# A second set of buffers for the turned probabilities, used in alternate steps

## The chip, the cores and the metric

The kernel runs on one core of a Trainium2 chip, as one launch. The metric is the device time of that core in microseconds (us), median of three runs. Lower is better.

## The reference, cut to what matters

The reference is a stack of four gated layers on a state x of 8 sequences of 112 tokens with 256 channels. Each layer does x = x + tanh(g) * attention(layernorm(x)) and then x = x + tanh(g) * ffn(layernorm(x)). The attentions look at a context of 375 tokens for each sequence:

```python
scores = q @ k.T * scale            # per head, 112 x 375
probs  = softmax(mask(scores))      # rows sum to one
out    = (probs @ v) @ w_o
```

- layer 0 (`a0`): 8 heads of 32 channels
- layer 1 (`a1`): 1 head of 128 channels
- layer 2 (`a2`): 16 heads of 16 channels; its feed-forward part holds two more self-attentions over the 112 tokens themselves (`af[0]`, `af[1]`), 16 heads of 16, causal, each followed by a mixture of experts
- layer 3 (`a3`): 16 heads of 64 channels

Everything is float32 except a quantized feed-forward part at the end. The feed-forward parts are not touched by the change.

## The kernel before, in words

The eight sequences are taken four at a time: four `LANES` (j = 0 to 3) make one iteration, and each attention runs two iterations (`it`). Every engine has its own program, and the order of work on each is written out by hand; semaphores (named `probs`, `probs_turned`, `probs_T`, ...) tie the engines together. An engine does its instructions strictly in the order written, so an instruction that waits holds back all that stand behind it on that engine.

An attention is cut into `tiles` of 128 channels (m), and a tile into `steps` (s); r = m * steps + s counts the steps through. One step takes one head of each of the four lanes (two heads a lane in `af`). The cross attentions have the following shapes: `a0` has 2 tiles of 4 steps, `a1` 1 tile of 1 step, `a2` 2 tiles of 8 steps, `a3` 8 tiles of 2 steps. Each `af` has 2 tiles of 4 steps. The work of a step r goes through these stations:

1. TensorE, `scores_of(r)` (L544): queries times keys, into PSUM banks 0 to 3, one for each lane.
2. VectorE, `mask_and_min(r)` (L668): adds the mask, writes the masked scores to SBUF (into `E` in even steps, `E_odd` in odd ones, so this buffer is already double) and finds the row minimum of the negated scores.
3. ScalarE, `exps(r, j)` (L749): the exponential in place, with the row sums.
4. TensorE, `turn_probs(r)` (L560): transposes the probabilities, 12 transposes of 112 x 125 (8 of 112 x 112 in `af`), into PSUM banks 4 to 6 (4 and 5 in `af`). It waits until the banks of step r - 1 were emptied.
5. ScalarE, `keep_probs(r)` (L761, in `af` L758), and VectorE, `keep_rest(r)` (L683): copy the turned probabilities from PSUM to SBUF, into `PT`. ScalarE takes two thirds of them (two copies of 125 x 448; one of 112 x 448 in `af`), VectorE the rest (one copy).
6. TensorE, `outputs_of(r)` (L584): turned probabilities times values, into PSUM bank 7. Its last matmul signals `probs_used`.

There is a single `PT`. So both copies of step r wait at station 5 for two signals: `probs_turned(r)`, and `probs_used(r - 1)`, which says that TensorE has read the turned probabilities of the step before.

The order on TensorE inside a tile is `outputs_of(r - 2)`, `scores_of(r + 1)`, `turn_probs(r)`, for each step (L602 to L609). In the last step of a tile it is `outputs_of(r - 2)`, then keys and queries of the next tile for two lanes (L491), `turn_probs(r)`, `outputs_of(r - 1)`, keys and queries for the other two lanes, `outputs_of(r)`, and the values of the next tile; in the last tile of an attention there is no next tile, and `turn_probs(r)`, `outputs_of(r - 1)`, `outputs_of(r)` follow each other with nothing between. After it come `turn_sums` (L592), the copy of the inverse row sums (L767), the scaling (L697) and the output projection (L491).

The order on ScalarE in a step is `exps(r, 0)`, `exps(r, 1)`, `keep_probs(r - 1)`, `exps(r, 2)`, `exps(r, 3)` (L773 to L781); in the last step of a tile `keep_probs(r)` stands behind them. The order on VectorE is `keep_rest(r - 1)`, `mask_and_min(r + 1)` (L709 to L712).

The buffers lie in one large SBUF tensor, `arena`, 4864 words for each lane, in which names share space when they are not in use at the same time; `stream` is a second tensor of 8192 words that holds weights in the expert stages, and in `a2` the values split by parity of the head (`V_keys`, its first 3072 words).

Of the kernel before, what the change touches and what calls it, by code (L numbers as in the profile page):

```python
# [28 lines left out]
S2 = 375  # L29
P = 128  # L30
# [62 lines left out]
class Attention:  # L93


    def __init__(self, tiles, heads, d, keys, key_tiles, wq, wk, wv, bq=None, bk=None, bv=None,
                 mask=None, guard=False, masked=None, by_parity=None, q_rows=None):
        self.tiles, self.heads, self.d, self.keys, self.key_tiles = tiles, heads, d, keys, key_tiles
        self.key_w = keys // key_tiles

        self.strip = max(32, d)
        self.strips = P // self.strip
        self.paired = d < 32
        self.whole_pairs = self.paired and key_tiles == 1
        self.group = 2 if self.whole_pairs else 1
        self.steps = heads // self.group
        self.stay = 2 if self.paired and not self.whole_pairs else 1
        self.wq, self.wk, self.wv, self.bq, self.bk, self.bv = wq, wk, wv, bq, bk, bv
        self.mask, self.guard, self.scale = mask, guard, float(d) ** -0.5
        self.masked, self.by_parity, self.q_rows = masked, by_parity, q_rows  # L110
# [16 lines left out]
def flamingo(nc, A, out):  # L127
    ctx = ExitStack()
    with ctx:
# [137 lines left out]
        PT_all, spread_all = lanes[:, :, off["p"]:off["p"] + 4 * T], lanes[0:T, :, off["s"]:off["s"] + P]  # L267
# [65 lines left out]

        def no_mask(j):
            return zero_col[0:T, :].broadcast_to([T, S2])

        a0 = Attention(2, 4, 32, S2, KEY_TILES, w_q0, w_k0, w_v0, "l0_bq", "l0_bk", row("l0_bv", KEY_W),
                       mask=no_mask, masked=twice)
        a1 = Attention(1, 1, 128, S2, KEY_TILES, w_q1, w_k1, w_v1, "l1_bq", "l1_bk", row("l1_bv", KEY_W),
                       mask=lambda j: maskb[0], guard=True, masked=twice)  # L340
        a2 = Attention(2, 8, 16, S2, KEY_TILES, w_q2, w_k2, w_v2, "l2_bq", "l2_bk", row("l2_bv", KEY_W),
                       mask=lambda j: maskb[j], masked=twice,
# [3 lines left out]
                        masked=lambda r, j: E[j][:, r % 2 * 2 * T:r % 2 * 2 * T + 2 * T], by_parity=V_rows)  # L346
              for l in range(2)]
        a3 = Attention(8, 2, 64, S2, KEY_TILES, w_q3, w_k3, w_v3, mask=no_mask, masked=twice)
# [155 lines left out]
        def attend_tensor(pe, a, p, it, rx, keys_of, keys_ready):  # L504
# [59 lines left out]
            def outputs_of(r):  # L564
# [10 lines left out]
                for first in range(0, LANES, a.strips):  # L575
                    for i in range(n):
                        for j in range(first, min(first + a.strips, LANES)):
                            t, rows = 0 if a.whole_pairs else i, a.rows(s, j)
                            if a.paired:
                                e, f = a.odd(s, i), t * P + rows.start  # L580
                                v = a.by_parity[j][0:a.key_w, e, f:f + a.strip]
                            else:
                                v = V[j][0:a.key_w, t, rows]
                            last = pe.matmul(outs[rows, j * T:(j + 1) * T], v, PT[j][0:a.key_w, i * T:(i + 1) * T],  # L584
                                             start=(i == 0 and s % a.stay == 0),
                                             stop=(i == n - 1 and s % a.stay == a.stay - 1))
# [43 lines left out]
        def attend_vector(v, a, p, it):  # L630
# [42 lines left out]
            def keep_rest(r):  # L673

                v.wait_ge(*p["probs_turned"].at(it, r))
                if r:
                    v.wait_ge(*p["probs_used"].at(it, r - 1))
                if a.whole_pairs:
                    dst, src = PT_all[0:T, 2:4, 0:2 * T], three(bank[5][0:T, 0:4 * T], 2)
                else:  # L680
                    n = a.key_tiles - 1
                    dst, src = PT_all[0:a.key_w, :, n * T:(n + 1) * T], three(bank[4 + n][0:a.key_w, 0:LANES * T], LANES)
# [48 lines left out]
        def attend_scalar(act, a, p, it):  # L731
# [21 lines left out]
            def keep_probs(r):  # L753
                act.wait_ge(*p["probs_turned"].at(it, r))
                if r:
                    act.wait_ge(*p["probs_used"].at(it, r - 1))
                if a.whole_pairs:
                    last = act.copy(PT_all[0:T, 0:2, 0:2 * T], three(bank[4][0:T, 0:4 * T], 2))  # L758
                else:
                    for t in range(a.key_tiles - 1):  # L760
                        last = act.copy(PT_all[0:a.key_w, :, t * T:(t + 1) * T],  # L761
# [1319 lines left out]
```

## Time and profile before

| | |
|---|---|
| median of 3 runs | 1913.39 us (1908.18 to 1920.59) |
| the profiled execution | 1915.56 us, of which the span of its instructions 1913.8 us |
| mean granted TensorE clock | 0.884 of full speed |
| TensorE busy (matmul) | 1534.9 us, 80% of the span |
| VectorE busy | 803.4 us, 42% |
| ScalarE busy | 674.3 us, 35% |
| GpSimd busy | 215.3 us, 11% |

The shares are means over stages that differ. By the trace the attentions lie as follows: `a0` from about 43 to 92 and 176 to 224 us, `a1` between 328 and 405, `a2` from 583 to 668 and 679 to 766, `af[0]` from 786 to 829 and 868 to 912, `af[1]` from 1162 to 1206 and 1252 to 1295, `a3` from 1446 to 1622 and 1642 to 1818 us. All the rest is projections, norms, experts and feed-forward parts. In rows of the timeline a bracket tells how long the engine had been idle before the instruction, and what ended the idle time.

### The profile page before, as it was taken

What the parts mean: (1) busy time and instruction counts of PE and PEld (TensorE: products, weight loads), DVE (VectorE), ACT (ScalarE), POOL (GpSimd) and SP (SyncE); (2) the same over time, 40 slices, a digit from 0 to 9 for tenths busy, and PEclk for the clock granted to TensorE, in tenths of its full rate; (3) what the DMA queues carried; (4) which work ended last, traced back from release to release, by engine and by line L of the source; (5) the groups of instructions that cost most, each with busy time, mean ns of one, the idle gap of its engine ahead of it and who ended that gap; (6) DMA issues with size and microseconds to landing.
All of it is one profiled execution on the core that took longest, in us unless ns stands there. A gap on an engine that the chain in (4) does not pass through costs nothing.

```text
span 1913.8 us, 34703 instructions
## 1 busy us (share of the span) xinstructions
PE 1534.9 (80%) x11511; PEld 1245.6 (65%) x11511; DVE 803.4 (42%) x2884; ACT 674.3 (35%) x2117; POOL 215.3 (11%) x326
## 2 busy tenths in 40 slices
PE   5977767879889889758469966487998999999954
PEld 4666655768776666536358955366896777787733
DVE  3545445441116565656301126563004443344456
ACT  2513413232106656426023325262333444244411
POOL 0000000000001111111221122014500000000000
PEclk9988988889999999867579988587999999999977
DMA  9300000128601100400169830112951001000000
GB/s 351 117 1 1 0 4 32 33 99 285 182 6 48 48 2 2 158 1 1 66 226 351 300 131 21 46 44 99 319 199 33 2 2 33 2 1 1 2 0 20
DMA packets 103092, 156.23 MB, mean 82 GB/s; under 512 B 12199, under 2 KB 80928, under 8 KB 102248
## 3 DMA queue, kind: packets, MB, share of 16 engines
q1 hardware_dynamic: 97355, 143.53, 22.7%
q0 software_dynamic: 3552, 9.18, 1.4%
q10 hardware_dynamic: 2048, 1.84, 0.3%
q8 instruction: 70, 1.15, 0.2%
q14 instruction: 67, 0.54, 0.1%
HBM read 147.31 MB, written 11.67 MB: 83 GB/s over the span
## 4 chain that ended last, share of the span: by engine, by line
PE 74%; DVE 8%; issue 6%; ACT 4%; DMA 4%; POOL 3%; SPq 1%; DVEq 1%; ACTq 0%; POOLq 0%
PE psum L491 51%; PE psum L560 8%; PE psum L584 6%; PE psum L544 5%; ACT arena L749 2%; DMA moe_b<-in_moe_b 2%; PE psum L479 2%; ACT arena L761 1%; SPq L889 1%; POOL rstd L461 1%; POOL stream L1111 1%; PE psum L592 1%; POOL token_rows L1083 1%; DMA region<-in_l_wv 1%; DVE x_state L823 1%
## 5 line engine op out<-in xcount | busy, mean ns | idle before, releaser
L491 PE MATMUL psum<-region,arena 128*125 128x128 f32 (+4 forms) x2160 | 372.7, 327 | 50.0 <-DVE arena L697 15.7
L491 PEld LDWEIGHTS psum<-region,arena 128*125 128x125 f32 (+2 forms) x2160 | 304.3, 191 | 113.5 <-issue 24.9
L749 ACT ACTIVATE arena<-arena,rowmin 112x375 f32<-112x375 f32 (+1 forms) x584 | 292.1, 505 | 187.4 <-DVE rowmin L668 187.1
L491 PE MATMUL psum<-arena,region 128*128 128x112 f32 (+2 forms) x1984 | 347.2, 335 | 4.2 <-DVE x_state L1738 1.7
L491 PEld LDWEIGHTS psum<-arena,region 128*128 128x128 f32 x1984 | 283.4, 205 | 69.3 <-issue 12.2
L560 PE MATMUL psum<-identity,arena 112*125 112x112 f32 (+1 forms) x1240 | 177.7, 287 | 30.9 <-ACT arena L761 14.8
L560 PEld LDWEIGHTS psum<-identity,arena 112*125 112x125 f32 (+1 forms) x1240 | 145.0, 180 | 87.1 <-ACT arena L761 26.6
L479 PE MATMUL psum<-identity,arena 112*128 112x112 f32 x176 | 39.0, 391 | 148.1 <-DVE arena L471 96.6
L491 PE MATMUL psum<-arena 128*128 128x128 f32 (+4 forms) x896 | 138.7, 313 | 0.5 <-DMA moe_b<-in_moe_b 0.5
L544 PE MATMUL psum<-arena 32*112 32x375 f32 (+3 forms) x912 | 134.8, 486 | 0.1
L491 PEld LDWEIGHTS psum<-arena 128*128 128x128 f32 (+2 forms) x896 | 124.7, 189 | 11.8 <-issue 0.9
L479 PEld LDWEIGHTS psum<-identity,arena 112*128 112x128 f32 x176 | 25.7, 198 | 163.4 <-DVE arena L471 102.9
L486 ACT COPY arena<-psum 128x224 f32<-128x224 f32 x80 | 27.5, 345 | 267.6 <-PE psum L479 265.2
L749 ACT ACTIVATION_READ_ACCUMULATOR arena<-arena,rowmin 112x1 f32 x584 | 111.6, 191 | 0.0
L683 DVE COPY arena<-psum 125x448 f32<-125x448 f32 (+1 forms) x114 | 71.1, 624 | 96.4 <-PE psum L584 92.6
L491 PE MATMUL psum<-arena,stream 128*128 (+1 forms) x832 | 100.1, 282 | 10.2 <-ACT arena L1208 3.4
L491 PEld LDWEIGHTS psum<-arena,stream 128*128 128x128 f32 x832 | 98.0, 198 | 14.6 <-issue 11.8
L805 POOL COPY arena<-rinv 112x128 f32<-112x128 f32 x136 | 33.9, 293 | 651.5 <-DVE rinv L688 623.7
L761 ACT COPY arena<-psum 125x448 f32<-125x448 f32 x164 | 79.3, 535 | 67.9 <-PE psum L584 56.6
L668 DVE CUSTOM_DVE_ANT_0 arena<-psum,zero_column 112x375 f32<-112x375 f32 x192 | 93.7, 544 | 15.3 <-PE psum L544 15.3
L584 PE MATMUL psum<-arena 125*64 125x112 f32 (+3 forms) x1712 | 91.6, 286 | 10.3 <-ACT arena L761 6.7
L1260 ACT ACTIVATE arena<-psum,moe_b 128x128 f32<-128x128 f32 x160 | 45.6, 368 | 129.6 <-PE psum L491 129.6
(220 smaller groups left out, 1598.0 us busy)
## 6 DMA issues: line engine op xcount, KB each, us to landing
stream<-in_moe_w SPq DMA_DIRECT2D x36, 1024.0 KB, 7.4
arena<-in_moe_w SPq DMA_DIRECT2D x36, 1024.0 KB, 7.4
arena<-in_ctxT SPq DMA_DIRECT2D x32, 375.0 KB, 3.8
stream<-in_e_wg SPq DMA_DIRECT2D x8, 512.0 KB, 4.7
stream<-in_e_wu SPq DMA_DIRECT2D x8, 512.0 KB, 5.8
stream<-in_e_wd SPq DMA_DIRECT2D x8, 512.0 KB, 6.7
region<-in_e_wg SPq DMA_DIRECT2D x8, 512.0 KB, 7.6
region<-in_e_wu SPq DMA_DIRECT2D x8, 512.0 KB, 8.4
```

Of the source, the lines that this page charges most:

```text
L479: last = pe.transpose(bank_t[j][:, c * T:(c + 1) * T], src[j][:, c * P:(c + 1) * P], ident[0:T, 0:T])
L486: act.copy(xT[j], three(bank_t[j][:, 0:2 * T], 2)).then_inc(p["xT_ready"].sem, 1)
L491: last = pe.matmul(dst, l, r, start=(i == 0), stop=(i == n - 1))
L544: pe.matmul(bank_s[j][0:T, 0:a.group * a.keys], lhs, rhs, start=True, stop=True)\
L560: last = pe.transpose(dst[0:a.key_w, n * T:(n + 1) * T], a.masked(r, j)[0:T, i * a.key_w:(i + 1) * a.key_w], ident[0:T, 0:T])
L584: last = pe.matmul(outs[rows, j * T:(j + 1) * T], v, PT[j][0:a.key_w, i * T:(i + 1) * T], start=(i == 0 and s % a.stay == 0), stop=(i == n ...
L668: last = nc.vector.tensor_tensor_reduce(out=a.masked(r, j)[0:T, ks], in0=bank_s[j][0:T, ks], in1=a.mask(j), scale=1.0, scalar=3.0e38, op0= ...
L683: v.tensor_copy(dst, src).then_inc(p["probs_rest_T"].sem, 1)
L749: last = act.activation(e, e, ACT.Exp, bias=rowmin[:, j, n:n + 1], scale=-1.0, accum_out=rowsum[:, j, h:h + 1])
L761: last = act.copy(PT_all[0:a.key_w, :, t * T:(t + 1) * T], three(bank[4 + t][0:a.key_w, 0:LANES * T], LANES))
L805: last = g.tensor_copy(three(spread[j], a.heads), rinv[:, j, 0:a.heads].unsqueeze(2).broadcast_to([T, a.heads, a.d]))
L1260: last = act.activation(tok_hid[r % 2][:, m * P:(m + 1) * P], bank[r % 2 * 2 + m // 4][:, m % 4 * P:(m % 4 + 1) * P], ACT.Gelu, bias=b1q[: ...
```

## The change

A second buffer for the turned probabilities is added, and steps take turns: an even step r writes and reads the old place, an odd one the new. Both copies now wait for `probs_used(r - 2)` in place of `probs_used(r - 1)`, and in steps 0 and 1 for none. Where the second buffer lies differs: in `a0` (and by name `a1`, which has one step only) in a part of `wide` of each lane; in `a2` and `a3` in `stream`, behind the split values; in `af`, whose turned probabilities are half as wide, in the second half of the old buffer. Number, shape and order of compute instructions and DMAs stay as they were.

```diff
-                 mask=None, guard=False, masked=None, by_parity=None, q_rows=None):
+                 mask=None, guard=False, masked=None, by_parity=None, q_rows=None, turned=None):
...
-        PT_all, spread_all = lanes[:, :, off["p"]:off["p"] + 4 * T], lanes[0:T, :, off["s"]:off["s"] + P]
+        PT_all = lanes[:, :, off["p"]:off["p"] + 4 * T]
+        PT_odd = [lanes[:, :, off["w"] + 2 * T:off["w"] + 5 * T],
+                  stream[:, 24 * P:24 * P + LANES * 3 * T].rearrange("p (j w) -> p j w", j=LANES)]
...
+        def turned_wide(r):
+            return PT_odd[0] if r % 2 else PT_all
+
+        def turned_stream(r):
+            return PT_odd[1] if r % 2 else PT_all
+
+        def turned_narrow(r):
+            return PT_all[:, :, r % 2 * 2 * T:r % 2 * 2 * T + 2 * T]
...
         a0 = Attention(2, 4, 32, S2, KEY_TILES, w_q0, w_k0, w_v0, "l0_bq", "l0_bk", row("l0_bv", KEY_W),
-                       mask=no_mask, masked=twice)
+                       mask=no_mask, masked=twice, turned=turned_wide)
...
-                            last = pe.matmul(outs[rows, j * T:(j + 1) * T], v, PT[j][0:a.key_w, i * T:(i + 1) * T],
+                            last = pe.matmul(outs[rows, j * T:(j + 1) * T], v, a.turned(r)[0:a.key_w, j, i * T:(i + 1) * T],
...
             def keep_rest(r):
 
                 v.wait_ge(*p["probs_turned"].at(it, r))
-                if r:
-                    v.wait_ge(*p["probs_used"].at(it, r - 1))
+                if r >= 2:
+                    v.wait_ge(*p["probs_used"].at(it, r - 2))
                 if a.whole_pairs:
-                    dst, src = PT_all[0:T, 2:4, 0:2 * T], three(bank[5][0:T, 0:4 * T], 2)
+                    dst, src = a.turned(r)[0:T, 2:4, 0:2 * T], three(bank[5][0:T, 0:4 * T], 2)
...
             def keep_probs(r):
                 act.wait_ge(*p["probs_turned"].at(it, r))
-                if r:
-                    act.wait_ge(*p["probs_used"].at(it, r - 1))
+                if r >= 2:
+                    act.wait_ge(*p["probs_used"].at(it, r - 2))
                 if a.whole_pairs:
-                    last = act.copy(PT_all[0:T, 0:2, 0:2 * T], three(bank[4][0:T, 0:4 * T], 2))
+                    last = act.copy(a.turned(r)[0:T, 0:2, 0:2 * T], three(bank[4][0:T, 0:4 * T], 2))
                 else:
                     for t in range(a.key_tiles - 1):
-                        last = act.copy(PT_all[0:a.key_w, :, t * T:(t + 1) * T],
+                        last = act.copy(a.turned(r)[0:a.key_w, :, t * T:(t + 1) * T],
                                         three(bank[4 + t][0:a.key_w, 0:LANES * T], LANES))
```

## Rows read from the trace of the kernel before

**Rows 1.** The page, part 4: the chain that ended last, by line.

```profile
PE psum L491 51%; PE psum L560 8%; PE psum L584 6%; PE psum L544 5%; ACT arena L749 2%; DMA moe_b<-in_moe_b 2%; PE psum L479 2%; ACT arena L761 1%; SPq L889 1%; POOL rstd L461 1%; POOL stream L1111 1%; PE psum L592 1%; POOL token_rows L1083 1%; DMA region<-in_l_wv 1%; DVE x_state L823 1%
```

**Rows 2.** Waits, whole span: who waited for whom, us in total, times, longest.

```profile
DVE arena L683 <- PE psum L584: 92.6, 80, 2.0
...
ACT arena L761 <- PE psum L584: 56.6, 56, 2.2
...
ACT arena L758 <- PE psum L584: 13.4, 14, 2.0
```

**Rows 3.** Busy by window (a2, af, a3): length, PE, PEld, DVE, ACT, POOL, clock, DMA.

```profile
600.00:675.00 75.00, 66.53 (x766) 48.52 (x764) 45.11 (x147) 52.24 (x151) 8.08 (x12) 0.98 0.11 32
...
1165.00:1206.00 41.00, 34.42 (x333) 23.71 (x332) 26.21 (x166) 29.03 (x138) 6.97 (x16) 0.85 0.01 2
...
1640.00:1820.00 180.00, 175.64 (x1393) 139.41 (x1394) 77.23 (x238) 75.03 (x204) 9.01 (x33) 0.99 0.01 1
```

**Rows 4.** Timeline, one inner step of a2: start us, length us, instruction, idle before.

```profile
600.67 0.79 PE L584 MATMUL psum<-arena,stream 125*32 125x112 f32 x24
...
601.39 0.90 PE L544 MATMUL psum<-arena 32*112 32x375 f32 x8
601.58 0.97 ACT L761 COPY arena<-psum 125x448 f32<-125x448 f32 x2 [0.29 <-PE psum L584]
...
602.42 0.55 DVE L668 CUSTOM_DVE_ANT_0 arena<-psum,arena 112x375 f32<-112x375 f32 x1 [0.20 <-PE psum L544]
...
602.61 1.76 PE L560 MATMUL psum<-identity,arena 112*125 112x112 f32 x12 [0.32 <-ACT arena L761]
...
604.30 0.79 PE L584 MATMUL psum<-arena,stream 125*32 125x112 f32 x24
...
604.72 0.19 ACT L749 ACTIVATION_READ_ACCUMULATOR arena<-arena,rowmin 112x1 f32 x1
...
605.21 0.97 ACT L761 COPY arena<-psum 125x448 f32<-125x448 f32 x2 [0.29 <-PE psum L584]
605.22 0.62 DVE L683 COPY arena<-psum 125x448 f32<-125x448 f32 x1 [0.84 <-PE psum L584]
```

**Rows 5.** Waits in 600 to 675 us, where a2 lies.

```profile
ACT arena L761 <- PE psum L584: 6.5, 14, 1.5
```

**Rows 6.** Waits in 43 to 92 us, where a0 lies.

```profile
ACT arena L761 <- PE psum L584: 4.2, 6, 1.5
```

**Rows 7.** Timeline, the end of the last tile of a2.

```profile
663.54 0.79 PE L584 MATMUL psum<-arena,stream 125*32 125x112 f32 x24
664.46 0.97 ACT L761 COPY arena<-psum 125x448 f32<-125x448 f32 x2 [1.48 <-PE psum L584]
...
665.48 0.79 PE L584 MATMUL psum<-arena,stream 125*32 125x112 f32 x24 [1.15 <-ACT arena L761]
```

**Rows 8.** Timeline, the end of the last tile of a3.

```profile
1617.24 1.39 PE L584 MATMUL psum<-arena 125*64 125x112 f32 x24
1618.72 0.97 ACT L761 COPY arena<-psum 125x448 f32<-125x448 f32 x2 [2.05 <-PE psum L584]
...
1619.75 1.38 PE L584 MATMUL psum<-arena 125*64 125x112 f32 x24 [1.12 <-ACT arena L761]
```

**Rows 9.** Timeline, the end of the last tile of af[0].

```profile
824.15 0.98 PE L584 MATMUL psum<-arena 112*32 112x112 f32 x16
825.24 0.53 ACT L758 COPY arena<-psum 112x448 f32<-112x448 f32 x1 [1.70 <-PE psum L584]
...
826.03 0.97 PE L584 MATMUL psum<-arena 112*32 112x112 f32 x16 [0.91 <-DVE arena L683]
```

**Rows 10.** Timeline, one copy of an inner step of af[1].

```profile
1198.86 0.53 ACT L758 COPY arena<-psum 112x448 f32<-112x448 f32 x1 [0.21 <-PE psum L584]
```

**Rows 11.** The chain in order of time, its longest pieces: start us, us, what.

```profile
91.79 6.67 PE psum L491 x16
...
1622.94 14.08 PE psum L491 x64
```

More of the change, by code:

```diff
@@ L109, in __init__ @@
         self.mask, self.guard, self.scale = mask, guard, float(d) ** -0.5
-        self.masked, self.by_parity, self.q_rows = masked, by_parity, q_rows
+        self.masked, self.by_parity, self.q_rows, self.turned = masked, by_parity, q_rows, turned
     def strip_of(self, s, j):
@@ L337, in flamingo @@
         a0 = Attention(2, 4, 32, S2, KEY_TILES, w_q0, w_k0, w_v0, "l0_bq", "l0_bk", row("l0_bv", KEY_W),
-                       mask=no_mask, masked=twice)
+                       mask=no_mask, masked=twice, turned=turned_wide)
         a1 = Attention(1, 1, 128, S2, KEY_TILES, w_q1, w_k1, w_v1, "l1_bq", "l1_bk", row("l1_bv", KEY_W),
-                       mask=lambda j: maskb[0], guard=True, masked=twice)
+                       mask=lambda j: maskb[0], guard=True, masked=twice, turned=turned_wide)
         a2 = Attention(2, 8, 16, S2, KEY_TILES, w_q2, w_k2, w_v2, "l2_bq", "l2_bk", row("l2_bv", KEY_W),
-                       mask=lambda j: maskb[j], masked=twice,
+                       mask=lambda j: maskb[j], masked=twice, turned=turned_stream,
                        by_parity=V_keys, q_rows=parity_q)
@@ L345, in flamingo @@
                         row2(l, "bv"), mask=lambda j: causal[:, :],
-                        masked=lambda r, j: E[j][:, r % 2 * 2 * T:r % 2 * 2 * T + 2 * T], by_parity=V_rows)
+                        masked=lambda r, j: E[j][:, r % 2 * 2 * T:r % 2 * 2 * T + 2 * T], by_parity=V_rows, turned=turned_narrow)
               for l in range(2)]
-        a3 = Attention(8, 2, 64, S2, KEY_TILES, w_q3, w_k3, w_v3, mask=no_mask, masked=twice)
+        a3 = Attention(8, 2, 64, S2, KEY_TILES, w_q3, w_k3, w_v3, mask=no_mask, masked=twice, turned=turned_stream)
         one = ("rstd_ready", "veps_ready")
@@ L675, in keep_rest @@
                 v.wait_ge(*p["probs_turned"].at(it, r))
-                if r:
-                    v.wait_ge(*p["probs_used"].at(it, r - 1))
+                if r >= 2:
+                    v.wait_ge(*p["probs_used"].at(it, r - 2))
                 if a.whole_pairs:
-                    dst, src = PT_all[0:T, 2:4, 0:2 * T], three(bank[5][0:T, 0:4 * T], 2)
+                    dst, src = a.turned(r)[0:T, 2:4, 0:2 * T], three(bank[5][0:T, 0:4 * T], 2)
                 else:
                     n = a.key_tiles - 1
-                    dst, src = PT_all[0:a.key_w, :, n * T:(n + 1) * T], three(bank[4 + n][0:a.key_w, 0:LANES * T], LANES)
+                    dst, src = a.turned(r)[0:a.key_w, :, n * T:(n + 1) * T], three(bank[4 + n][0:a.key_w, 0:LANES * T], LANES)
                 v.tensor_copy(dst, src).then_inc(p["probs_rest_T"].sem, 1)
```

## The prediction

> **What bounds the kernel now.** I read the chain of work that ended last first. TensorE's projections (L491) hold half of it, and the lines of the attentions that the change touches hold little: L560 8%, L584 6%, L544 5%, and the copy that is to start earlier, L761, 1% [rows 1]. So the whole effect must fit into small gaps. The waits come next. VectorE's copy waits 92.6 us for `outputs_of`, ScalarE's 56.6 us in the cross attentions and 13.4 us in `af` [rows 2]. These are the waits that the second buffer takes away, but idle time on an engine that isn't the bound is worth nothing. Which of it is worth something must be read stage by stage.
>
> The busy times by window sort the stages [rows 3]. In `a3` TensorE is busy 175.6 of 180 us: it is the bound, and it does not wait for the copies inside. In `a2` it is busy 66.5 of 75 us and ScalarE 52.2, so there the engines take turns. One inner step of `a2` shows how [rows 4]. ScalarE's copies start at 601.58 and the next ones at 605.21: the step takes 3.62 us. Going round: `outputs_of` starts at 600.67, and `scores_of` follows at 601.39. The copy, idle for 0.29 us until L584 is done, starts 0.19 us later; it ends at 602.55, and TensorE, idle for 0.32 us on ScalarE, starts turning at 602.61. `outputs_of` of the next step comes at 604.30. That is the ring: turn, outputs, copy, turn. The outputs are in the ring only because there is one buffer. ScalarE was finished with its exponentials at 604.91 (604.72 + 0.19) and could have copied then, since the turned probabilities were complete before 604.30. It waited for 0.3 us.
>
> **The change, part by part.** No compute instruction and no DMA is added, removed or moved in its queue, so SP and POOL issue what they did. Per attention iteration only the two waits of step 1 fall away; the later ones ask for an older value. I cost that at nothing. Another address of the same shape costs nothing either.
>
> *Inner steps, `a2` and `a0`.* Without the wait ScalarE is never idle in the step, and the step takes ScalarE's own work: 3.62 - 0.29 = 3.33 us. Would something else stop it? TensorE needs 0.72 (outputs) + 0.90 (scores, 602.61 - 601.39 less 0.32 idle) + 1.69 (turning, 604.30 - 602.61) = 3.31 us, and the last of these already holds waits for exponentials. That just fits, and it is the cover that this step rests on. VectorE has 0.84 + 0.20 us idle in each step, so after 0.29 it still has 0.75. All from [rows 4]. The next thing late is then the exponentials themselves.
>
> How many steps count? `a2` shows 14 such waits in an iteration and 6.5 us [rows 5]. Two of the 14 are the copies that end a tile (about 1.5 us each), which leaves 12 of 0.29. A copy counts where TensorE's next turn waits for it. In the first tile the sixth copy is not waited for, since 16 projection matmuls stand between; so 5 + 6 = 11. `a0` has 6 waits and 4.2 us [rows 6]: two of them end tiles, and of the remaining four the second of the first tile is hidden in the same way, leaving 3. With two iterations each: 2 x (11 + 3) = 28 steps x 0.29 = **8.1 us**. Bounds: 0 if another engine takes over the 0.29, and 0.32 each (9.0) by TensorE's own gap.
>
> *The end of an attention.* There `turn_probs(r)`, `outputs_of(r - 1)`, copy of r, `outputs_of(r)` stand in a row with nothing between, and TensorE idles 1.15 us in `a2` [rows 7]. With two buffers the copy runs beside `outputs_of(r - 1)`. It starts 0.2 to 0.3 us after TensorE passes to the next group (0.19 in [rows 4]), that is at 663.54 + 0.3 = 663.84 instead of 664.46, so `outputs_of(r)` starts 0.62 earlier. `a0` has the same shapes: 4 ends x 0.62 = **2.5 us**. In `a3` `outputs_of(r - 1)` lasts 1.39 us, longer than the copies' 0.97 [rows 8]; the whole 1.12 us of TensorE's idle time goes: 2 x 1.12 = **2.2 us**. In `af` TensorE waits 0.91 us [rows 9]. There VectorE's copy is the later one, and at 824.45 + 0.62 it is ready about when TensorE is, so the 0.91 go: 4 x 0.91 = **3.6 us**. What follows (turned sums, scaling, projection) hangs on `outputs_of(r)` and moves with it. Bounds: nothing if the inverse sums from GpSimd become the late ones, 4 x 1.15 + 2 x 1.12 + 4 x 0.91 = 10.5 us if every gap closes.
>
> *Inner steps of `af`.* ScalarE has eight exponentials in a step and is mostly never idle; of the 14 waits of L758 four are the ends above, four more close first tiles and lie behind projections, and six are short. I count 5 waits of 0.21 as in [rows 10], **1.0 us**. Bounds 0 and 1.3.
>
> *Inside `a3`, and `a1`:* nothing. TensorE is full in the one [rows 3]; its 8 long waits of ScalarE per iteration are covered by projections, except the last. The other has a single step.
>
> Sum: 8.1 + 2.5 + 2.2 + 3.6 + 1.0 = **17.4 us**. Against the profiled execution's own 1915.56 us (span 1913.8 and 1.8 around it) that is 1898.2. It lay 2.2 us above the median, so for the median I forecast 1913.4 - 17.4 = **1896 us**. By the bounds: 0 to 20.8 us.
>
> **The rivals.**
>
> *A new wait takes the place of the old in the inner steps (1904 us).* TensorE's 3.31 and ScalarE's 3.33 us are all but equal, and they hang on each other: the last transposes of a step wait for the exponentials behind the copy. If each waits in turn, the 0.29 comes back as another gap. Then 17.4 - 8.1 = 9.3 us remain, 1904. Against it: part of the 1.69 us is such waiting already and shrinks with the step. Chance 0.14.
>
> *The clock stays up behind the attentions (1890 us).* Behind the end of `a0` 16 projection matmuls took 6.67 us, while behind `a3` 64 took 14.08, or 3.52 for 16 [rows 11]. The first ran at half clock (1.2 GHz), after a stretch in which TensorE had stood still more than it worked. The change closes part of these gaps. At most 4 x 3.15 = 12.6 us are to be had behind `a0` and `a2`; with half of it, 6.3, the time is 1890. Chance 0.14.
>
> *The clock falls inside the inner steps (slower, 1938 us).* All inner steps of `a2` ran at a granted clock of 0.98 [rows 3]. If a shifted beat let it fall to 1.2 GHz, TensorE's 3.31 us would become up to 6.6, 3.0 more than now; twenty-four matmuls of `outputs_of` take 0.79 us at full clock, sixteen took 0.98 in `af` at half [rows 4, 9]. It decides from about 6 such steps on (17.4 / 3.3); with one iteration of `a2`, 14 steps, it is 1896 + 42 = 1938. Against it: TensorE becomes busier per us, not idler. The Trainium skill ("TensorE: Matmul & The Clock Gate", Part 4, PE-mode transpose) speaks for it: transposes do not count as TensorE work for the gate, and half of a step's TensorE time is transposes. By that rule alone the inner steps would already be at half clock; the trace of this kernel shows 0.98 there, so I follow the row. Chance 0.03.
>
> *It doesn't do what it says (1913 us):* the wait named was not the real one, and ScalarE was held by `probs_turned` or its own queue. Against it: the copies follow L584 by the same distance in every step. Chance 0.03.
>
> **How the numbers follow.** The forecast has 0.66, with a range of its own of 1889 to 1903, from the terms and the spread of the runs (12.4 us with nothing changed). A measurement of this kernel can tell about 1% from no change, that is 1894.3 and 1932.5 us. The forecast lies just inside: of its 0.66 I put 0.22 below 1894.3. With 0.12 from the case of the clock that makes 0.34 faster, 0.63 within 1%, 0.03 slower. Range for 8 in 10: 1886 to 1906; it takes in the case of the new wait and most of the case of the clock, and leaves out the last two.
>
> **What would show it.** Inner steps of `a2`: copies of L761 3.33 us apart, no idle time before them, and TensorE's gap on L761 before L560 near zero. Ends: in `a2` the copy 0.2 to 0.3 us after the start of L584 and not 0.9; in `a3` no gap between the two groups of L584. In `a3` tiles as long as now, though the waits of L761 on L584 vanish there too. The prediction is wrong if the copies stay 3.62 apart, or if the granted clock of the windows in [rows 3] moves by more than 0.03.

## The result, and the profile after

The changed kernel takes **1895.63 us** (median of 6 runs, 1885.55 to 1898.06). The kernel before, run beside it, takes 1912.9 us (median of 6, 1908.18 to 1920.59). The ratio is **0.9892, 95% interval 0.9860 to 0.9925**, about 21 us gained. The forecast was 1896. Run again later beside other kernels, it had 1888.17 us against 1915.0, a ratio of 0.9855 [0.9832, 0.9878].

The profiled execution took 1894.89 us, with a span of 1893.3 (before 1913.8) and a mean granted clock of 0.881 (before 0.884). So the 20.5 us between the two spans do not come from a higher clock on the whole. In the changed kernel's file the lines stand a little lower: L491 is now L502, L544 is L555, L560 is L571, L584 is L595, L668 is L679, L683 is L694, L749 is L760, L758 is L769, L761 is L772.

The chain that ended last, by line (part 4 of the page), answers to [rows 1]:

```profile
PE psum L502 52%; PE psum L571 7%; PE psum L555 5%; PE psum L595 5%; ACT arena L760 3%; DMA moe_b<-in_moe_b 2%; PE psum L490 2%; SPq L900 1%; POOL rstd L472 1%; POOL stream L1122 1%; PE psum L603 1%; DMA arena<-expert_out 1%; DMA region<-in_l_wv 1%; DVE x_state L834 1%; ACT arena L772 0%
```

The copy (L772) fell from 1.3% to 0. Turning (L571) fell from 7.7 to 6.8% and outputs (L595) from 5.7 to 5.1%, while the scores (L555) rose from 4.7 to 5.5%. The exponentials (L760) rose from 1.9 to 2.9%, in time from 36 to 54 us: 8 us of these 54 lie in `a0`, where they had none before, and all the rest in `af`.

The waits of the whole span (total us, times, longest) no longer list the copies behind the outputs [rows 2]. What is left for the copies is waiting for the turning, in short pieces. VectorE's first wait here stood at 98.8 us before; it grew by 20 us, and no stage became longer by it:

```profile
DVE arena L652 <- ACT arena L748: 119.0, 64, 3.1
...
ACT stream L772 <- PE psum L571: 15.9, 20, 0.8
```

An inner step of `a2` in the timeline (start, length, idle before) answers to [rows 4]:

```profile
599.68 0.94 ACT L772 COPY stream<-psum 125x448 f32<-125x448 f32 x2
...
602.38 0.78 PE L595 MATMUL psum<-stream 125*32 125x112 f32 x24
...
602.79 0.62 DVE L694 COPY arena<-psum 125x448 f32<-125x448 f32 x1
602.80 0.20 ACT L760 ACTIVATION_READ_ACCUMULATOR arena<-arena,rowmin 112x1 f32 x1
602.89 0.95 ACT L772 COPY arena<-psum 125x448 f32<-125x448 f32 x2
...
603.10 0.90 PE L555 MATMUL psum<-arena 32*112 32x375 f32 x8
...
603.92 1.75 PE L571 MATMUL psum<-identity,arena 112*125 112x112 f32 x12
604.12 0.55 DVE L679 CUSTOM_DVE_ANT_0 arena<-psum,arena 112x375 f32<-112x375 f32 x1 [0.71 <-PE psum L555]
...
605.60 0.79 PE L595 MATMUL psum<-arena,stream 125*32 125x112 f32 x24
...
619.47 1.47 PE L571 MATMUL psum<-identity,arena 112*125 112x112 f32 x12
620.88 0.79 PE L595 MATMUL psum<-arena,stream 125*32 125x112 f32 x24
```

From copy to copy it is 602.89 - 599.68 = 3.21 us, where it was 3.62. The copy has no idle time before it, so ScalarE's own work fills the step. On TensorE no gap shows either: 0.72 + 0.82 + 1.68 = 3.22 us, start to start. But the 1.68 us of turning are not all work. Behind a projection, where the exponentials are long ready, the same twelve transposes take 620.88 - 619.47 = 1.41 us (the last two rows). So some 0.27 us of waiting for exponentials hide in the turning, and TensorE's own work is about 2.95 us. The buffers alternate (`stream`, `arena`). The copy starts at 602.89, 0.09 us after the last part of the exponentials *started* (602.80), and before that part has ended.

The ends of the attentions, `a2` first, then `a3`, then `af[0]`, answer to [rows 7 to 9]:

```profile
657.58 0.79 PE L595 MATMUL psum<-arena,stream 125*32 125x112 f32 x24
657.68 0.97 ACT L772 COPY stream<-psum 125x448 f32<-125x448 f32 x2 [0.67 <-PE psum L571]
...
658.71 0.78 PE L595 MATMUL psum<-stream 125*32 125x112 f32 x24 [0.34 <-ACT stream L772]
...
1599.85 1.38 PE L595 MATMUL psum<-arena 125*64 125x112 f32 x24
1599.96 0.97 ACT L772 COPY stream<-psum 125x448 f32<-125x448 f32 x2 [0.67 <-PE psum L571]
1601.07 1.32 PE L595 MATMUL psum<-stream,arena 125*64 125x112 f32 x24
...
811.25 1.85 PE L595 MATMUL psum<-arena 112*32 112x112 f32 x32
811.36 0.53 ACT L769 COPY arena<-psum 112x448 f32<-112x448 f32 x1 [0.49 <-PE psum L571]
811.36 0.62 DVE L694 COPY arena<-psum 112x448 f32<-112x448 f32 x1
```

The copies start 0.10 to 0.11 us after TensorE has passed on. Between the two groups of outputs lie 1.13 us in `a2` (before 1.94) and 1.22 in `a3` (before 2.51). In `af[0]` the 32 matmuls run as one group, so all of TensorE's 0.91 us of waiting is gone.

Busy times by window, of `a2` and `a3` (columns as in [rows 3]):

```profile
594.00:669.00 75.00, 68.58 (x800) 50.65 (x792) 48.56 (x162) 54.24 (x159) 10.75 (x14) 0.99 0.11 32
...
1620.00:1800.00 180.00, 175.48 (x1391) 138.90 (x1392) 77.21 (x238) 74.98 (x204) 9.02 (x33) 0.99 0.01 1
```

Whole stages tell the sum better than windows. A stage is taken here from the start of its first 36 matmuls of keys and queries to the start of the projection behind its end, both from the chain in order of time. For the first iteration of `a2` and of `a3` these are, before the change (the end of `a3` stands in [rows 11]) and after it:

```profile
591.11 4.13 PE psum L491 x36
...
668.09 5.28 PE psum L491 x16
...
1457.85 4.12 PE psum L491 x36
```

```profile
589.60 4.12 PE psum L502 x36
...
661.30 3.72 PE psum L502 x16
...
1440.56 4.12 PE psum L502 x36
...
1604.20 14.08 PE psum L502 x64
```

| stage (us) | before | after | difference, all iterations |
|---|---|---|---|
| `a0`, first and second iteration | 48.17, 48.15 | 46.14, 46.13 | -4.05 |
| `a2` | 76.98, 76.97 | 71.70, 71.70 | -10.55 |
| `a3` | 165.09, 165.09 | 163.64, 163.64 | -2.90 |
| `af`, four stages together | 184.93 | 180.57 | -4.36 |

Together that is 21.9 us; the span became 20.5 shorter, so all that lies outside of these stages gave back 1.4. This is itself a balance. The four projections directly behind `a0` and `a2` took 6.0 us less in this profiled run, and the rest 7.4 more; 4.5 of these lie in the second iteration of `a1` and the 30 us behind it, which took 55.6 us at a granted clock of 0.66 where it had 51.1 at 0.77. The three cross attentions repeat to 0.02 us from one iteration to the next. The `af` stages do not: they spread from 43.3 to 46.4 after and from 45.5 to 47.5 before, with a granted clock between 0.79 and 0.89. In five other profiled runs, of kernels in which at least one of the two copies at the ends of `af` still waits for the step before, the four take 179.8 to 187.6 us. So the 4.36 us of the last row are within what these stages differ by anyway; what the change is worth there must be read from parts of them at a like clock (see the account of the prediction).

### The profile page after: what moved, and what is told of

Same layout as the page of the kernel before. It is cut to its first block, busy times and chain, and to the rows that moved or that the text cites. A ratio compares the mean times of both kernels' runs of the same rounds, so it can differ in the third digit from the quotient of the medians.

```text
span 1893.3 us, 34683 instructions
## 1 busy us (share of the span) xinstructions
PE 1533.7 (81%) x11511; PEld 1250.5 (66%) x11511; DVE 799.7 (42%) x2884; ACT 670.1 (35%) x2117; POOL 215.3 (11%) x326
## 4 chain that ended last, share of the span: by engine, by line
PE 74%; DVE 7%; issue 7%; ACT 5%; DMA 3%; POOL 2%; SPq 1%; DVEq 1%; ACTq 0%; POOLq 0%
PE psum L502 52%; PE psum L571 7%; PE psum L555 5%; PE psum L595 5%; ACT arena L760 3%; DMA moe_b<-in_moe_b 2%; PE psum L490 2%; SPq L900 1%; POOL rstd L472 1%; POOL stream L1122 1%; PE psum L603 1%; DMA arena<-expert_out 1%; DMA region<-in_l_wv 1%; DVE x_state L834 1%; ACT arena L772 0%
## 5 line engine op out<-in xcount | busy, mean ns | idle before, releaser
L502 PE MATMUL psum<-region,arena 128*125 128x128 f32 (+4 forms) x2160 | 368.5, 325 | 50.1 <-DVE arena L708 15.7
L502 PEld LDWEIGHTS psum<-region,arena 128*125 128x125 f32 (+2 forms) x2160 | 302.4, 190 | 111.1 <-issue 23.6
L760 ACT ACTIVATE arena<-arena,rowmin 112x375 f32<-112x375 f32 (+1 forms) x584 | 292.8, 508 | 189.5 <-DVE rowmin L679 189.5
L502 PE MATMUL psum<-arena,region 128*128 128x112 f32 (+2 forms) x1984 | 352.9, 339 | 3.7 <-DVE x_state L1749 1.7
L502 PEld LDWEIGHTS psum<-arena,region 128*128 128x128 f32 x1984 | 288.4, 209 | 69.5 <-issue 12.1
L571 PEld LDWEIGHTS psum<-identity,arena 112*125 112x125 f32 (+1 forms) x1240 | 144.5, 180 | 74.7 <-ACT arena L760 21.7
L571 PE MATMUL psum<-identity,arena 112*125 112x112 f32 (+1 forms) x1240 | 175.3, 285 | 21.4 <-ACT arena L769 6.6
L502 PE MATMUL psum<-arena 128*128 128x128 f32 (+4 forms) x896 | 137.9, 312 | 1.4 <-DMA moe_b<-in_moe_b 1.4
L555 PE MATMUL psum<-arena 32*112 32x375 f32 (+3 forms) x912 | 135.2, 490 | 0.1
L502 PEld LDWEIGHTS psum<-arena 128*128 128x128 f32 (+2 forms) x896 | 124.2, 189 | 12.5 <-issue 1.8
L760 ACT ACTIVATION_READ_ACCUMULATOR arena<-arena,rowmin 112x1 f32 x584 | 113.4, 194 | 0.0
L502 PE MATMUL psum<-arena,stream 128*128 (+1 forms) x832 | 100.5, 283 | 9.7 <-ACT arena L1219 3.4
L502 PEld LDWEIGHTS psum<-arena,stream 128*128 128x128 f32 x832 | 98.4, 198 | 13.9 <-issue 11.3
L679 DVE CUSTOM_DVE_ANT_0 arena<-psum,zero_column 112x375 f32<-112x375 f32 x192 | 93.9, 544 | 18.7 <-PE psum L555 18.6
L1271 ACT ACTIVATE arena<-psum,moe_b 128x128 f32<-128x128 f32 x160 | 45.6, 368 | 129.1 <-PE psum L502 129.1
L502 PE MATMUL psum<-stream,arena 128*112 128x256 f32 (+1 forms) x352 | 80.3, 379 | 0.0
L555 PEld LDWEIGHTS psum<-arena 32*112 32x112 f32 (+2 forms) x912 | 57.1, 176 | 31.3 <-DVE rowmin L679 4.4
L679 DVE CUSTOM_DVE_ANT_0 arena<-psum,arena 112x375 f32<-112x375 f32 x136 | 67.0, 544 | 19.3 <-PE psum L555 18.8
```

Source lines behind the costliest of these rows:

```text
L502: last = pe.matmul(dst, l, r, start=(i == 0), stop=(i == n - 1))
L555: pe.matmul(bank_s[j][0:T, 0:a.group * a.keys], lhs, rhs, start=True, stop=True)\
L571: last = pe.transpose(dst[0:a.key_w, n * T:(n + 1) * T], a.masked(r, j)[0:T, i * a.key_w:(i + 1) * a.key_w], ident[0:T, 0:T])
L679: last = nc.vector.tensor_tensor_reduce(out=a.masked(r, j)[0:T, ks], in0=bank_s[j][0:T, ks], in1=a.mask(j), scale=1.0, scalar=3.0e38, op0= ...
L760: last = act.activation(e, e, ACT.Exp, bias=rowmin[:, j, n:n + 1], scale=-1.0, accum_out=rowsum[:, j, h:h + 1])
L1271: last = act.activation(tok_hid[r % 2][:, m * P:(m + 1) * P], bank[r % 2 * 2 + m // 4][:, m % 4 * P:(m % 4 + 1) * P], ACT.Gelu, bias=b1q[: ...
```

## The experiments

**The theory:** the gain lies at the copies that TensorE's next group waits for, and it comes from the longer leash. "Leash" stands here for how far back the outputs lie that a copy waits for: one step (r - 1, short) or two (r - 2, long). Rivals: the second buffer's place or address matters; VectorE's wait, the longest of those that the change takes away, is the one that counts; the time comes from TensorE's clock behind the attentions.

**Buffers without the longer leash.** Both copies use the two buffers, but still wait for `probs_used(r - 1)`:

```diff
-                if r >= 2:
-                    v.wait_ge(*p["probs_used"].at(it, r - 2))
+                back = 1
+                if r >= back:
+                    v.wait_ge(*p["probs_used"].at(it, r - back))
...
```

The same edit is made on ScalarE. (This diff and those below are against the changed kernel.)

> Both buffers stay and steps alternate between them, but both copies wait for probs_used(r - 1) again. If the whole gain comes from the shorter waits, this is the kernel before: inner steps of a2 3.62 us apart, 0.29 us idle on ScalarE before each, 1.94 us between the two last groups of outputs_of, about 1913 us (1908 to 1920). If it came from where the buffers lie (other addresses for the copies and for TensorE's reads), part of the 17 to 20 us stays: steps under 3.6, under 1905 us.

Measured: 1914.78 us, one run, beside 1915.48 for the kernel before. Stage `a2` 76.93, copies 3.62 apart:

```profile
601.43 0.97 ACT L774 COPY stream<-psum 125x448 f32<-125x448 f32 x2 [0.29 <-PE psum L595]
...
605.05 0.97 ACT L774 COPY arena<-psum 125x448 f32<-125x448 f32 x2 [0.29 <-PE psum L595]
```

In `a0` (48.16, 48.14) and `a2` the place costs and brings nothing. Each iteration of `a3` takes 164.98 us here, and 164.97 to 164.99 in every other kernel with two buffers and a short leash on ScalarE's last copy; the kernel before has 165.09. Those 0.11 us are not the leash's. All the rest of the effect in these stages is.

**The long leash on ScalarE's copy alone** (VectorE waits for r - 1).

> Only ScalarE's copies get the longer leash (r - 2); VectorE's copy waits for probs_used(r - 1) as before. If ScalarE's wait was all that counted, inner steps of a2 take 3.21 us as in the changed kernel, and the time is 1893 to 1898. If VectorE's copy becomes the late one: it starts 0.92 after outputs_of, takes 0.62, and turning starts 0.06 later, 1.60 after outputs_of; with 1.68 for turning the step is about 3.28, and at the ends of a0 and a2 1.6 instead of 1.13 lies between the two groups of outputs_of. Then 28 x 0.34 + 4 x 0.34 + 2 x 0.34 + 4 x 0 = 11.6 us gain, about 1901.

Measured: 1897.7 us, one run. Stage `a2` 72.35, that is 4.6 of the 5.3 us of an iteration. I had expected steps of 3.28; they are 3.21, as short as with both:

```profile
600.17 0.78 PE L595 MATMUL psum<-stream 125*32 125x112 f32 x24
600.69 0.95 ACT L773 COPY arena<-psum 125x448 f32<-125x448 f32 x2
601.09 0.62 DVE L695 COPY arena<-psum 125x448 f32<-125x448 f32 x1 [0.43 <-PE psum L595]
601.82 1.65 PE L571 MATMUL psum<-identity,arena 112*125 112x112 f32 x12
...
603.90 0.95 ACT L773 COPY stream<-psum 125x448 f32<-125x448 f32 x2
...
657.14 0.78 PE L595 MATMUL psum<-stream 125*32 125x112 f32 x24 [0.91 <-DVE stream L695]
```

In the inner steps VectorE's copy still waits 0.43 us, ends at 601.71, and makes the turning about 0.1 us late (1.13 us after ScalarE's copy in place of 1.03). That delay is not passed on: the turning takes 1.57 us to the next group in place of 1.68, because 0.27 us of the 1.68 were waiting for exponentials anyway. What is missing of the stage is the end, where VectorE's short leash holds the last copy (the last row: TensorE idle for 0.91 us on it).

**The long leash on VectorE's copy alone.**

> Only VectorE's copy gets the longer leash; ScalarE waits for probs_used(r - 1) as before. ScalarE's two copies (0.97) end after VectorE's one (0.62), so nothing moves in a0, a2 and a3: steps 3.62 us, 1.94 us between the last groups, about 1912 us; in af VectorE's copy was the later at the ends, 4 x 0.1 there. If VectorE's wait of 92.6 us had been the costly one, most of the gain would be here: under 1903 us.

Measured: 1907.62 us in one run, which looked like a gain of 8, while stage `a2` (76.91) and `a0` had not moved. So I ran it again, timed:

> The kernel of the run in which only VectorE's copy got the longer wait, now timed. Theory (in the cross attentions a step is bound by ScalarE's leash; VectorE's alone returns nothing there, and what that single run gained lay in the clock of the stages around): inner steps of a2 stay 3.62 us apart, stage a2 76.9, a0 48.15, a3 unchanged; by these nothing is gained. In af VectorE's copy is the later one at the ends (0.1 behind ScalarE's), so at most 4 x 0.1 there: time within 0.3% of the kernel before, 1909 to 1918 us. Rival (VectorE's leash is worth something in af, where TensorE's groups wait for both copies): af's four stages together at 180 us again where before had 184.9, and a time of 1905 to 1910 us, a ratio whose interval lies below 1.

Measured: 1916.61 us (12 runs) beside 1917.71 (17 runs), ratio 0.9993 [0.9976, 1.0009]. `a2` 76.92, `a0` 48.16. Here VectorE's copy goes first, without any wait, and in these steps nobody profits:

```profile
602.30 0.79 PE L595 MATMUL psum<-arena,stream 125*32 125x112 f32 x24
602.41 0.62 DVE L694 COPY stream<-psum 125x448 f32<-125x448 f32 x1
603.21 0.97 ACT L773 COPY stream<-psum 125x448 f32<-125x448 f32 x2 [0.29 <-PE psum L595]
604.23 1.76 PE L571 MATMUL psum<-identity,arena 112*125 112x112 f32 x12 [0.31 <-ACT stream L773]
```

The longer of the two copies' waits, 92.6 us on VectorE [rows 2], is worth next to nothing by itself. Only at the ends of `af`, where VectorE's copy is the later one, do the two groups of outputs move together, from 1.88 to 1.68 us in all four: 0.8 us of 1915, more than the 0.4 expected, and too little for the timing to show. The 8 us of the single run were in the main the spread between runs: of the twelve the fastest has 1909.91.

**The long leash inside only, and at the ends only.** The first kernel waits for r - 1 in the last step of an attention and for r - 2 elsewhere, the second the other way round (its line reads `back = 2 if ... else 1`). Both copies are edited alike:

```diff
-                if r >= 2:
-                    act.wait_ge(*p["probs_used"].at(it, r - 2))
+                back = 1 if r == a.tiles * a.steps - 1 else 2
+                if r >= back:
+                    act.wait_ge(*p["probs_used"].at(it, r - back))
...
```

> The longer leash in all steps but the last of each attention, which waits for probs_used(r - 1). By the theory of the ring: inner steps of a2 and a0 3.21 us instead of 3.62, 28 of them, 11.5 us, and about 1 in af; 1.94 us stay between the last two groups of outputs_of. 1913 - 12.5 = 1900 us. By the rival that the clock behind the attentions gave a good part of the gain: the 16 projection matmuls behind the first end of a0 take 3.7 us here too and the time is under 1898.

> The longer leash in the last step of each attention alone. Inner steps of a2 stay at 3.62 us. Ends: between the last two groups of outputs_of 1.13 us instead of 1.94 in a0 and a2, 1.22 instead of 2.51 in a3, 0.9 instead of 1.88 in af: 4 x 0.81 + 2 x 1.29 + 4 x 0.98 = 9.7 us, 1903 us. The two parts add up to 22 us if they are independent. By the rival of the clock: with the gaps of the ends closed, the projection behind the first end of a0 runs at full clock (3.7 us for 16 matmuls, not 6.67), and some us more are won: under 1900.

| | time (us), ratio [95%] | `a0` | `a2` | `a3` | `af`, four together |
|---|---|---|---|---|---|
| before | 1916.9 | 48.17 | 76.98 | 165.09 | 184.93 |
| inside only (4 runs) | 1898.2, 0.9881 [0.9847, 0.9916] | 46.95 | 72.53 | 164.98 | 183.41 |
| ends only (10 runs) | 1906.98, 0.9945 [0.9926, 0.9964] | 47.36 | 76.12 | 163.64 | 184.66 |
| both (the change) | see the result | 46.14 | 71.70 | 163.64 | 180.57 |

(The stages are those of the profiled runs; the row before has the time of the runs beside these kernels and the stages of the first profile.)

The stages of the cross attentions add up. In `a2` the inner steps bring 4.45 = 11 x 0.405 and the end 0.86, together 5.31; the change brought 5.28. In `a0` it is 1.22 = 3 x 0.41 and 0.81. That confirms the count of 11 and 3 steps, and so does where the gain lies: in the first tile of `a2`, before any end, the changed kernel is 2.03 us ahead, 5 x 0.41. The times do not add up as well: the ratio of the inside kernel means 22.8 us [16.1, 29.3], while its stages in the profiled run are only some 13 us shorter. That profiled run (1903.72) is the longest of its four. What the others saved outside of the stages has no trace and stays open. For the ends-only kernel the stages are 6.5 us shorter, with next to nothing from `af`: the four second tiles, where the ends lie, took 4.6 us less than before, the first tiles 5.4 us more, two of them at a granted clock of 0.78 where before had 0.92.

**More work taken from ScalarE in `a0` and `a2`.** With the wait gone ScalarE's own 3.21 us set the step, so one of its two copies goes to VectorE, in one copy of two banks. `shared(r)` is true in the inner steps of `a0` and `a2`:

```diff
+            def shared(r):
+                return not a.whole_pairs and a.steps > 2 and r % a.steps < a.steps - 1
...
+                if shared(r):
+                    dst = a.turned(r)[0:a.key_w, :, T:3 * T].rearrange("p j (t w) -> p t j w", t=2)
+                    src = psum[0:a.key_w, 5:7, 0:LANES * T].rearrange("p t (j w) -> p t j w", j=LANES)
...
-                    for t in range(a.key_tiles - 1):
+                    for t in range(1 if shared(r) else a.key_tiles - 1):
...
```

> On top of the change: in the inner steps of a0 and a2 VectorE copies two of the three banks in one instruction (125 x 896), ScalarE one. If ScalarE's own work (4 x 0.59 + 0.84) is now what sets the step of 3.21 us, it falls to the next bound: ScalarE 2.8, VectorE 4 x 0.47 + 0.08 + about 1.1 = 3.06, TensorE 0.72 + 0.82 + 1.40 = 2.94, so about 3.06 and 28 x 0.15 = 4 us less than the changed kernel, 1891 us. If TensorE or the semaphores between the engines set it, the step stays at 3.2 or grows, and the time is 1896 or more.

Measured: 1888.5 us (4 runs), ratio 0.9853 [0.9831, 0.9875]; the plain change beside it had 0.9855 [0.9832, 0.9878]. No difference in the time; stage `a2` 71.02 and 70.98 in place of 71.69. The work taken off ScalarE turned into waits for VectorE:

```profile
601.07 0.61 ACT L766 ACTIVATE arena<-arena,rowmin 112x375 f32<-112x375 f32 x1 [0.50 <-DVE rowmin L679]
...
602.36 1.09 DVE L700 COPY arena<-psum 125x896 f32<-125x896 f32 x1
...
603.55 1.53 PE L571 MATMUL psum<-identity,arena 112*125 112x112 f32 x12 [0.16 <-issue]
```

The exponentials wait 0.50 us for the masks (first row), and the turning starts at 603.55, 0.10 us after VectorE's long copy ends (602.36 + 1.09). From one group of outputs to the next the steps alternate between 3.24 and 3.04 us, 3.14 in the mean, where 3.06 had been expected. TensorE's own 2.95 us were not the limit. In every second step VectorE is: its four masks and the long copy take 3.03 us, from one step's first mask (600.48) to the next one's (603.51), without a wait between them. That the two iterations of `a0` and of `a2` are 1.5 us shorter together is too little to show in the time.

**ScalarE's copy of `af` to VectorE.** There the step is 3.40 us before and after, and ScalarE is full with eight exponentials and a copy:

```diff
                 if a.whole_pairs:
+                    if r % a.steps < a.steps - 1:
+                        v.tensor_copy(a.turned(r)[0:T, 0:2, 0:2 * T], three(bank[4][0:T, 0:4 * T], 2))\
+                            .then_inc(p["probs_T"].sem, 1)
...
```

(and `keep_probs` returns at once in these steps.)

> On top of the change: in the inner steps of af VectorE makes both copies and ScalarE none (at the ends they share as before). ScalarE's eight exponentials and a copy take 3.40 us a step there; without the copy 8 x 0.374 = 2.99. VectorE has 8 x 0.195 + 2 x 0.6 = 2.8. If ScalarE is the bound of these steps, five of them count in each of the four iterations: up to 20 x 0.4 = 8 us, less where TensorE at half clock takes over (about 3.3 us a step): 3 to 8 us less than the changed kernel, 1890 us. If the ring through turning is the bound, no gain, or a loss of 2 to 4 us, since two copies follow each other on one engine.

> The two moves of work to VectorE together. If both hold and are independent, 4 + 5 = 9 us less than the changed kernel, 1887 us; if either makes VectorE the bound, 1893 or more.

> The changed kernel again, on the same chip as the three before, to compare them with: ratio 0.989 to 0.991 of the kernel before, about 1895 us.

| on one chip, before at 1915.0 | time (us) | ratio to before [95%] |
|---|---|---|
| the change (4 runs) | 1888.17 | 0.9855 [0.9832, 0.9878] |
| with `af`'s copy moved (5 runs) | 1875.12 | 0.9788 [0.9771, 0.9804] |
| with both moves (5 runs) | 1873.3 | 0.9782 [0.9759, 0.9804] |

The second move adds nothing that can be told. The first brings more than the 3 to 8 us that I had expected: the four stages of `af` fell from 179.67 to 166.46, by 13.2. The timeline of the same two steps, first the change again, then with the copy moved:

```profile
798.02 0.59 PE L595 MATMUL psum<-arena 112*32 112x112 f32 x16
799.59 0.60 PE L571 MATMUL psum<-identity,arena 112*112 112x112 f32 x4 [0.40 <-ACT arena L769]
...
801.42 0.59 PE L595 MATMUL psum<-arena 112*32 112x112 f32 x16
```

```profile
797.36 0.60 PE L595 MATMUL psum<-arena 112*32 112x112 f32 x16
...
800.33 0.59 PE L595 MATMUL psum<-arena 112*32 112x112 f32 x16
801.95 1.66 PE L571 MATMUL psum<-identity,arena 112*112 112x112 f32 x8 [1.02 <-DVE arena L697]
```

A step takes 2.97 us in place of 3.40. Part of the 13.2 us is clock: the granted clock in these stages was 0.90 to 0.94 where the change had 0.84 to 0.85. 3.0 of the 13.2 us lie before a stage's first scores, where no copy of `af` stands. The other 10.2 lie in the tiles. Three inner steps in each of eight tiles would make 24 x 0.43 = 10.3 us. But tiles at a like clock show less: a first tile took 20.04 us in the one stage of the changed kernel that had it at full clock and 19.04 to 19.42 with the copy moved, a second tile 18.65 and 17.0 to 17.5 (at 0.82 to 0.87 and at 0.86 to 0.90). That makes about 9 us for the move, a little more than I had expected, and about 4 for the clock.

**The moved copy with the short leash** (r - 1 everywhere, otherwise the kernel just told).

> Both copies in the inner steps of af on VectorE as in the run that moved them, two buffers, but every copy waits for probs_used(r - 1) as in the kernel before. Tells whether the 13 us of the moved copies need the second buffer. Theory A (the gain comes from freeing ScalarE, the bound of af's inner steps; the wait for the outputs before is then still in the ring, about 0.3 us a step): inner steps of af 2.9 to 3.0 us where the moved copies with the long leash had 2.6 to 2.7, af's four stages together about 174 to 177 us (24 inner steps x 0.3 = 7, ends 4 x 0.9 = 3.6 above 166.5), a2 76.9, a0 48.15, a3 as before; time 1913 - 17 + (13 - 10) ... worked out: before 1915, minus about 8 to 10 in af, so 1902 to 1908. Rival B (VectorE's copies come after its masks anyway, so the outputs before are long read and the long leash returns nothing in the inner steps): inner steps 2.6 to 2.7, af's stages 170 us, time about 1899 to 1902.

Measured: 1906.06 us, ratio 0.9935 [0.9914, 0.9956]. In time that is where theory A put it; the four stages of `af`, 180.3 us, lie beyond what either had (174 to 177, 170). In the inner steps rival B is right. In the first two stages they are as short as with the long leash:

```profile
813.72 0.59 PE L595 MATMUL psum<-arena 112*32 112x112 f32 x16
...
816.69 0.59 PE L595 MATMUL psum<-arena 112*32 112x112 f32 x16
817.42 0.62 DVE L692 COPY arena<-psum 112x448 f32<-112x448 f32 x1 [0.27 <-PE psum L595]
...
818.82 1.63 PE L571 MATMUL psum<-identity,arena 112*112 112x112 f32 x8 [1.53 <-DVE arena L698]
820.38 0.97 PE L595 MATMUL psum<-arena 112*32 112x112 f32 x16
822.26 0.97 PE L595 MATMUL psum<-arena 112*32 112x112 f32 x16 [0.91 <-DVE arena L698]
```

2.97 us again. (The 2.6 to 2.7 in both expectations was the distance of one pair of turnings, not a whole step; that part of both missed.) So the two edits don't need each other inside: the move is worth 0.43 a step, the leash nothing there. At the end of the attention the short leash costs twice. TensorE waits 0.91 us for the last copy (the last row). And one step earlier VectorE's two copies start only at 817.42, 0.73 us after the outputs before them, where with the long leash they start 0.23 after; so the last turning comes 2.13 us after the outputs in place of 1.62 (801.95 - 800.33). That is 0.5 us more, which both expectations left out. Of the four stages two ran at a granted clock of 0.90 and took 43.1 us each, the other two at 0.75 and 0.84 and took 48.4 and 45.6.

## Why the prediction was right, and where it was lucky

**The place and the mechanism hold.** The ring of the inner step, the ends and the count of 28 steps are as forecast, shown by the buffers-only kernel (nothing in `a0` and `a2`) and by the two halves (4.45 and 0.86 in `a2`).

**The inner steps were undersized.** I took 0.29 us a step, ScalarE's idle time, and forecast a step of 3.33 us; measured are 3.21, a gain of 0.41 a step and 28 x 0.41 = 11.5 us in place of 8.1. The idle time is counted from the end of one instruction to the start of the next. But without a wait ScalarE's next instruction starts before the last has ended: 0.09 us after the start of a 0.20 us one. The Trainium skill says so too ("Perfetto Trace Analysis", Optimizing Scalar/DVE Operations): the half of an instruction's latency in which its write is acknowledged overlaps with the next instruction, some 93 ns for ScalarE on SBUF. The trace has 0.11 us for it (0.20 - 0.09). In [rows 4] the last exponential's part starts at 604.72, so a free copy would have started at 604.81, and it started at 605.21: 0.40 us. The same row held the right number; I read the wrong difference. My upper bound of 0.32, TensorE's gap, was wrong too: with the gap gone the scores took 0.82 us to the turning where I had counted 0.90. The cover was also wider than I thought: of the 3.31 us that I gave TensorE, about 2.95 are its own (turning 1.41 in place of 1.69).

**The ends were undersized** for a like reason. I let the copy start 0.2 to 0.3 us after TensorE passes on; it starts at 0.10. In `a0` and `a2` that makes 0.81 and 0.86 in place of 0.62, 3.3 us in place of 2.5. In `a3` the copy's cover is complete: 2.51 - 1.22 = 1.29 at the group, 1.34 over the stage (164.98 inside only, 163.64 ends only), where I had 1.12.

**`af` came out near the sum for its ends alone.** Whole stages spread by 3 us and cannot tell. The second tile, from the turned sums behind the first (L603) to the projection, can: it took 19.44 to 19.66 us in the inside-only kernel (granted clock 0.78 to 0.85) and 18.64 to 18.65 in the changed kernel when it was run again (0.82 to 0.87). That is 1.0 for each end, 4.0 us on the 3.6 that I had. The 1.0 for the inner steps has no support: at full clock the step is 3.40 us before and after. The short waits of [rows 10] bring nothing visible, since ScalarE is full there.

**The sum.** By the rows: 11.5 + 3.3 + 2.7 + 4.0 = 21.5 us in place of 17.4. The span shows 20.5, the ratio of the medians 21 [14, 27] and, in the later comparison, 28 [23, 32]. With the right sizes I would have said 1913.4 - 21.5 = 1891.9, which lies between the two medians, 1895.63 and 1888.17. So part of how near 1896 came to the first is luck. I had held a change within 1% for the likeliest, with 0.63; at 0.9892 and 0.9855 both comparisons lie on the far side of that bound, the first with an interval that reaches across it. It was above all the undersized inner step that put the forecast on the near side.

**The rivals.** *A new wait* did not come: ScalarE fills the step with 3.21 us, and TensorE's own 2.95 leave room for the waiting that hides in its turning. VectorE's masks wait 0.71 us there, which hurts nobody. *The clock stays up behind the attentions* looked true at first, since the projection behind `a0` took 3.69 us in place of 6.67. But with VectorE's leash alone, where TensorE's gap at the end stayed, it was 3.69 as well; with closed ends and nothing else it was 5.38; and in the inside-only kernel it was 3.69 in one iteration and 6.69 in the other, behind stages that took 46.95 and 46.94. The four projections behind `a0` and `a2` took 22.53, 16.33, 17.98, 16.51, 19.51 and 19.33 us in the six profiled runs with TensorE's gaps at these ends as before (mean 18.7), and 16.51 (four times), 19.89 and 18.20 in the six with ends closed (mean 17.4). (With the long leash on ScalarE alone, which closes the gaps in part, it was 17.66.) The 6.3 us of that rival are not there; whether 1 us is can't be said. *The clock falls inside the inner steps* is refuted by the granted clock of 0.99 in `a2`. By the rule of the Trainium skill on transposes ("TensorE: Matmul & The Clock Gate", Part 4, PE-mode transpose), taken alone as in the prediction, these steps, with 1.68 of 3.21 us of turning, would run at half clock; the trace shows 0.98 before and 0.99 after. What I named as a sign against me, a window's clock that moves by more than 0.03, did not happen in `a2` and `a3`; for `af` the sign was a poor one, since its stages differ by more than that within a run. *It doesn't do what it says* is refuted by the waits.

## What to carry to other kernels

What a removed wait returns is the time from where the instruction would have started behind its predecessor's start, not the idle time that the trace prints. A long wait in the list is worth nothing if another one releases the same successor later: of two copies behind one turn, only the one that ends last counts, and the 92.6 us wait was the wrong one. Once a ring is broken, ask which engine is full in the new step and move work off it only where the others have room: one moved copy brought about 9 us in `af` (13 with the clock), while in `a2` VectorE became the late one in its place and the time did not move. And read a stage's gain between fixed points at a like clock: whole stages of `af` hid what their second tiles show.

## What the runs showed of the hardware

- Successive ScalarE instructions overlap by about 0.1 us: a copy started 0.09 us after the start of a 0.20 us instruction. A wait for another engine takes this away.
- A copy that waits for TensorE's turning starts 0.10 to 0.11 us after the start of TensorE's next group.
- Twelve transposes of 112x125 took 1.40 us (before) and 1.41 us (after) from their start to the next group's where no exponentials were awaited, and 1.68 us in an inner step of `a2`.
- The same 16 matmuls behind `a0` took between 3.69 and 6.72 us, in kernels whose stage before them differed by 2 us or not at all, and 3.69 and 6.69 in the two iterations of one run. So one profiled run can show a gain of 3 us there that is not the change's.
- With 0.84 to 0.85 of the clock granted, the four `af` stages took 179.67 us; with 0.90 to 0.94 and the copy moved, 166.46.
